# Softmax denominators of a two-layer graph kernel summed in batches of four steps, with six score buffers

## The reference

```python
h = maximum(layernorm(x), 0)
Wh, We = h @ W, entity_embs @ W
scores = (Wh @ a1)[:, None] + (We @ a2)[None, :]          # 4096 x 4096
e = where(scores > 0, scores, 0.2 * scores)
e = where(adj > 0, e, -9e15)
x = x + elu(softmax(e, axis=1) @ entity_embs + h)
h = maximum(layernorm(x), 0)
x = x + ((adj == 1).astype(x.dtype) @ h + h)
```

## Time and profile before

| | |
|---|---|
| median of 3 runs | 390.28 us (387.43 to 391.92) |
| profiled execution, first to last instruction (span) | 385.5 us; the profile gives no other time of this execution |
| PE matmuls busy | 345.7 us, 90% |
| DVE busy | 301.8 us, 78% |
| ACT busy | 193.1 us, 50% |
| POOL busy | 116.9 us, 30% |
| mean granted TensorE clock | 0.991 of full speed |

### The profile page before, as it was taken

How to read it: one execution, slowest core, us unless ns; L and a number is a source line. 1 busy time by engine, 2 the same in 40 slices (tenths; PEclk the granted TensorE clock), 3 DMA queues, 4 the chain that set the end, 5 groups by cost and what they waited for, 6 DMA issues and landing times. The chain is left out here.

```text
span 385.5 us, 5795 instructions
## 1 busy us (share of the span) xinstructions
PE 345.7 (90%) x2375; PEld 125.6 (33%) x2375; DVE 301.8 (78%) x331; ACT 193.1 (50%) x265; POOL 116.9 (30%) x160
## 2 busy tenths in 40 slices
PE   1598896999867989998998999989999999999996
PEld 0355331223211222332322323322224233335564
DVE  2826969998889999999899788899997999622211
ACT  1122635776466569635657765346567565412100
POOL 4870841111111124145211611102017697001400
PEclk9989899999999999999999999999999999999999
DMA  6999999999696976746899679999999960000011
GB/s 212 258 214 212 215 214 213 214 213 214 127 148 116 156 135 131 127 92 111 123 145 158 99 133 103 108 86 96 108 103 106 103 65 0 2 0 2 2 54 56
DMA packets 15849, 47.93 MB, mean 124 GB/s; under 512 B 1552, under 2 KB 1616, under 8 KB 15568
## 3 DMA queue, kind: packets, MB, share of 16 engines
q0 software_dynamic: 14656, 44.05, 73.8%
q1 hardware_dynamic: 1168, 3.52, 2.5%
HBM read 111.53 MB, written 1.05 MB: 292 GB/s over the span
## 5 line engine op out<-in xcount | busy, mean ns | idle before, releaser
L670 ACT ACTIVATE yp<-yp,tbias 128x1024 f32<-128x1024 f32 (+1 forms) x160 | 150.9, 975 | 101.4 <-DVE yp L897 100.4
L897 DVE SCALAR_TENSOR_TENSOR yp<-s8b,t8neg,am 128x1024 f32<-128x1024 f32 (+1 forms) x160 | 164.6, 1079 | 6.9 <-PE pb L1224 5.8
L1203 PE MATMUL pb<-yp,enta 128*64 128x512 f32 x512 | 136.2, 616 | 21.8 <-ACT yp L670 21.7
L809 DVE TENSOR_TENSOR am<-am,vx 128x4096 uint16<-128x4096 uint16 x32 | 73.7, 2304 | 1.6 <-ACT vx L564 1.2
L436 POOL DMA_DIRECT2D am<-adj_t x64 | 34.8, 562 | 123.4 <-DVE yp L897 123.1
L1224 PE MATMUL pb<-yp,onesf 128*32 128x512 f32 x512 | 68.2, 605 | 0.0
L1203 PEld LDWEIGHTS pb<-yp,enta 128*64 128x64 f32 x512 | 28.4, 136 | 87.1 <-ACT yp L670 53.6
L1115 PE MATMUL pb<-am,h 128*64 128x512 bf16 (+1 forms) x432 | 55.1, 379 | 0.0
L1115 PEld LDWEIGHTS pb<-am,h 128*64 128x64 bf16 x432 | 26.3, 110 | 39.5 <-issue 28.7
L445 POOL DMA_DIRECT2D am<-adj_t x16 | 11.4, 715 | 60.5 <-DVE yp L897 60.5
L1115 PE MATMUL pa<-am,h 128*64 128x512 fp8e4 x240 | 28.2, 380 | 0.0
(11 more groups left out here) (160 smaller groups left out, 245.7 us busy)
## 6 DMA issues: line engine op xcount, KB each, us to landing
am<-adj_t POOLq DMA_DIRECT2D x80, 512.0 KB, 11.6
edge<-adj_t POOLq DMA_DIRECT2D x4, 512.0 KB, 9.9
enta<-ent SPq DMA_DIRECT2D x1, 1040.0 KB, 5.1
xs<-xt SPq DMA_DIRECT2D x1, 1024.0 KB, 11.5
out<-yp SPq DMA_DIRECT2D x4, 256.0 KB, 2.0
mats<-eye SPq DMA_DIRECT2D x1, 320.0 KB, 7.0
wt_sb<-w_t SPq DMA_DIRECT2D x1, 32.0 KB, 2.1
a_sb<-a_cols SPq DMA_DIRECT2D x1, 0.5 KB, 2.0
```

The lines of the kernel that those rows point to most:

```text
L670: e = sc.activation(y, y, ACT.Exp, bias=tbias[:, at:at + 1])
L809: v.tensor_tensor(at, at, vx[:, pair(b) % 2, cols(b)].bitcast(U16).unsqueeze(1).to_broadcast([P, 2 * tiles(b), width(b)]), ALU.bitwise_xor ...
L897: y = v.scalar_tensor_tensor(out=yp[:, n % YS, r * HALF:r * HALF + W], in0=s8b[:, pair(b) % 2, cols(b)], scalar=t8neg[:, at:at + 1], in1=a ...
L1203: t.matmul(acc2(b)[s * D:(s + 1) * D, :], enta[:, at, 0:D], yp[:, n % YS, s * HALF:(s + 1) * HALF], start=(jt == 0), stop=final, tile_posi ...
```

## The change

`YS` is 6 in place of 5. The denominators are summed after every step with jt % 4 = 3, for the last four steps, in two groups of four matmuls with `pv_done` incremented by 2 behind each group. What stood at odd jt with jt % 4 = 1 is gone from there, and its wait for `den_sb` (or for `h0_ready` in block 0) stands at jt = 3 in place of jt = 1.

```diff
-YS = 5
+YS = 6
+BATCH = 4
...
-                if jt % 2 == 1:
-
-                    if jt == 1:
+                if jt % BATCH == BATCH - 1:
+
+                    if jt == BATCH - 1:
                         if b >= 1:
                             pe.wait_ge(den_sb, 2 * b)
                         else:
                             pe.wait_ge(h0_ready, 2)
-                    for r in range(2):
-                        for s in range(2):
-                            at = r * D + s * 32
-                            mm = t.matmul(dens[at:at + 32, :], onesf[:, 0:32],
-                                          yp[:, (n - 1 + r) % YS, s * HALF:(s + 1) * HALF],
-                                          start=(jt == 1), stop=final, tile_position=(0, at))
-                    mm.then_inc(pv_done, 2)
+                    for n2 in range(n - BATCH + 1, n + 1, 2):
+                        for r in range(2):
+                            for s in range(2):
+                                at = r * D + s * 32
+                                mm = t.matmul(dens[at:at + 32, :], onesf[:, 0:32],
+                                              yp[:, (n2 + r) % YS, s * HALF:(s + 1) * HALF],
+                                              start=(jt == BATCH - 1 and n2 + BATCH == n + 1), stop=(final and n2 + 1 == n),
+                                              tile_position=(0, at))
+                        mm.then_inc(pv_done, 2)
```

## The result

The changed kernel takes 392.8 us (median of 9 runs, 391.88 to 394.33), the kernel before, run beside it, 389.25 us (387.43 to 391.92). The ratio is 1.0101, with a 95% interval of 1.0073 to 1.0128: slower by 1%. The profiled execution took 392.17 us, of which 390.1 us are its span, against 385.5 for the span of before. So the medians are 3.55 us apart and the two profiled spans 4.6: the execution of before that was profiled was the fastest of its nine (387.43), and that of the changed kernel lay near its median.

A forecast was written before the change was run, and what follows sets the result against it. The prediction had the bound change hands between PE and DVE (with ACT behind it); -2.3 - 0.8 + 3.3 + 0 = +0.2 us gave 385.7 in the profiled execution's terms, 390.5 at the median, range 385.0 to 395.0.

The forecast's parts named there:

- the third rival: Blocks 1 to 4: coarser buffer release delays one score tile per batch, +5.6 us on the sum, 396 us; chance 0.13.
- the first rival: All 32 removed groups on PE each save 0.28 us, 9.0 in all; with the new wait 384.6 us; chance 0.14.
- Where PE sets the pace: PE time saved counts only at 72.4-97.5, 139.5-167.1, 203.5-244.9 and 281.7 us to the end; -2.3 us.
- An excursion is 0.28 us, and 17 of 32 give nothing: PE's change to 32-column form and back costs 0.28 us; the 17 removed groups directly ahead of L1012 save 0.
- The score bounds come earlier, -0.3 and -0.5: Postponed groups let a block's last L1012 come earlier, at 167.07 us (-0.3) and 244.93 us (-0.5); -0.8 us.
- The new wait, +3.3: End of block 1: DVE's lone_rows waits for pv_done = 30, reached later; L818 starts at 117.25, not 113.98; +3.3 us.
- The second rival: The new wait at the end of block 1 is taken up by later slack: 387.2 us; chance 0.12.
- The coarser release costs nothing with six buffers: Score tiles: denominators free buffers in larger batches, costing 0; DVE's waits on pv_done stay under 8 us.
- The clock: PE's idle over 4 us near 118 to 122 might halve the clock; counted as nothing in the sum.
- The fourth rival: Half clock for some 3 us behind PE's gap costs 1.5 to 2 us, partly hidden: 391 to 392.5; chance 0.11.

The follow-up runs named there:

- experiment 1: Changed kernel, but DVE's lone_rows waits for its own semaphore, lone_done, in place of pv_done: 386.06 us, ratio 0.9892 to the kernel before.
- experiment 7: Changed kernel with lone_rows on its own semaphore, and block 4 summing its denominators every second step again: 388.26 us, ratio 0.9989.
- experiment 2: Kernel before with one number changed: lone_rows of block 2 waits for pv_done = 32 in place of 30: 394.76 us, ratio 1.0131.
- Experiment 3: Changed kernel, wait kept, with 14 thrown-away matmuls in PE's gap right before the product of step 32: 389.32 us, ratio 0.9986.
- experiments 8 and 9: Changed kernel with batches at jt % 4 = 1, directly ahead of L1012: 392.76 us; the same with two gaps filled by thrown-away matmuls: 393.26 us.

## Why the prediction was right, and where it was not

The forecast was 390.5 us and no clear difference, in a range of 385 to 395. The measured 392.8 lies in the range, and the ratio of 1.0101 (1.0073 to 1.0128) is clear of no change by about the 1% at which the prediction drew its line. Part of this is luck. In the profiled executions the sum said +0.2 us and +4.6 came. The range held that because its upper end was drawn for another mechanism, the third rival's. (Its lower end, 385.0, doesn't quite reach the first rival's own 384.6.) And the 390.5 stands on a median of three runs, 390.28, that nine runs put at 389.25. By its steps:

- *Where PE sets the pace.* Held at the end: the gain of 2.0 us came in the last stretch. Between 139 and 167 us PE had no gap, but nothing in hand either. In experiment 1 PE had one group less to do there and soon waited 0.93 us for an exponential (the row at 152.92 below), which before had ended just in time.
- *An excursion is 0.28 us, and 17 of 32 give nothing.* The size held: 8.31 to 8.03 us in four steps, -2.0 us in block 4 as predicted, +2.2 when put back (experiment 7). The rule of the drain taken alone, the first rival, would have given 9 us in all; the version without the wait gained 2.7. That the 17 give nothing fits the rows: the second half of a batch adds 0.86 us (1.85 less 0.99), and a group ahead of L1012 takes 0.88 away. No run tested it alone.
- *The score bounds come earlier, -0.3 and -0.5.* Half right. In the profile of experiment 1 DVE was 0.17 us late at 205.91 and 0.69 early at 254.84, so the first gain didn't come (+0.4 between 132 and 206 in place of -0.3) and the second was 0.86. The bounds' last group at the first place, in the kernel before, and the timeline of experiment 1 towards it:

```profile
166.41 0.61 PE L1012 MATMUL pa<-am,gtab 128*32 128x512 bf16 x8
```
```profile
152.92 1.08 PE L1206 MATMUL pb<-yp,enta 128*64 128x512 f32 x4 [0.93 <-ACT yp L672]
...
164.27 2.48 DVE L899 SCALAR_TENSOR_TENSOR yp<-s8b,t8neg,am 128x1024 f32<-128x1024 f32 x2 [1.62 <-PE pb L1228]
...
168.08 0.62 PE L1014 MATMUL pa<-am,gtab 128*32 128x512 bf16 x8
```

With 1.70 us taken off, the bounds' last group stands at 166.38: not earlier, since the gap of 0.93 us had used up the group saved. DVE came 0.2 us later than before, behind tiles that had waited 1.62 us for the batch.

- *The new wait, +3.3.* Held, its place and its queue too: L819 started at 117.23 for the 117.25 forecast. Two small errors met in that: the batch began at 116.03, 0.22 us earlier than the 116.25 taken, and DVE started 1.20 us behind its first matmul in place of 1.0. The wait alone costs 3.5 us (experiment 2). The second rival, that slack takes it up, fell.
- *The coarser release costs nothing with six buffers.* Nearly held: DVE's waits for the denominators in the score tiles went from 5.8 to 7.8 us, six of them in place of eight, below the 8 us named. But it wasn't free where DVE follows close behind PE: the wait of 1.62 us at 164.27 above stands ahead of the late shifts.
- *The clock.* This is the step that failed: its fall stood in the sum at nothing. The prediction had the gap ("PE is idle for over 4 us near 118 to 122"), but held the fall behind it for a rival of 0.11 and hid part of its price in PE's later gaps. The clock did fall, in the changed kernel and in experiment 2, and the whole 2.2 us reached DVE. The slow product delays the normalisation of the first blocks, which runs over PE, ACT and DVE by turns. The changed kernel's timeline shows the two waits through which it came:

```profile
129.06 0.71 DVE L829 STREAM_TRANSPOSE gmax<-rows 64x512 f32<-64x512 f32 x1 [0.73 <-ACT rows L586]
...
135.07 0.69 DVE L840 TENSOR_TENSOR ta<-num,pa 128x512 f32<-128x512 f32 x1 [1.54 <-PE pa L1077]
```

Experiment 3, with the clock held, has no wait at the first of these places and 0.20 us at the second. PE's gaps there are no cover, for PE stands idle only because DVE is late. Nor did the prediction count a second fall, 1.6 us. The fourth rival's time, 391 to 392.5, was the nearest of all, with one fall in it and not two.

The sum as measured, in the profiled executions: -0.2 (up to 102), +3.5 (the wait, from -0.22 to +3.25), +2.2 (first fall), -0.5 (the middle without the falls: +0.4 and -0.9), +1.6 (second fall), -2.0 (block 4): +4.6. The forecast had, in the same order, -0.3, +3.3, nothing, -0.8, nothing and -2.0.

The Trainium skill, TensorE: Matmul & The Clock Gate, section HAM oscillation, has idle gaps between bursts of matmuls bring the slow clock back. The trace agrees for the gap of 4.51 us here and of 5.37 us in experiment 2; the gap of 1.90 us at the same place in the kernel before brought none. In experiment 3, with the same wait of 4.50 us but matmuls run in the gap, so that its last part is 1.38 us, none came either.

## What to carry to other kernels

When a group of work that increments a counter is postponed, list every wait on that counter, and not only those of the buffers it was made for: one old wait at a block's end, asking for a count that had always been there in time, turned a gain of 1% into a loss of 1%. Give such a wait the semaphore of the very work it guards. And price a new gap on TensorE together with the slower clock behind it, at its full size if a chain over several engines follows: here the gap's 3.5 us became 5.7 (experiment 2, on the ruler). A stretch in which an engine has no gap is not yet one in which its saved time counts: the inputs must be there earlier than they are used, or the saving turns into a wait.

## What was not expected of the hardware

The fall of the clock lasted longer than the gap that brought it: from about 121 to almost 128 us, between 6 and 7 us at half speed, behind 4.5 us of idle, with PE at work from 122.46 on. And a fall also came at a gap of only 1.44 us, at 209.40, and at the same gap in experiments 8 and 9, where the kernel before and experiments 1 to 3, with the same gap, kept their clock. So in these traces the length of the last gap alone doesn't say whether the clock falls.
